# A two-layer graph/FFN kernel on one core: gate, experts and transposes at other steps of the adjacency pass

## What is computed

```python
h = item_feat @ W_item.T + b_item
b = layernorm(x) @ W_user.T + b_user
x = x + relu(adj @ h + b)
xf = layernorm(x)
probs = softmax(xf @ gate_w + gate_b)          # 8 experts
cw = the two largest probs of each row, else 0
for e in range(8):
    y = gelu(xf @ W1[e] + b1[e]) @ W2[e] + b2[e]
    out += cw[:, e:e+1] * y
x = x + out
```

## Time and profile before

| | |
|---|---|
| median of 3 runs | 1682.82 us |
| the profiled execution | 1680.87 us |
| its span, first to last instruction | 1679.0 us |
| TensorE, matmuls | 1617.9 us, 96% of the span |
| TensorE, weight loads | 1314.1 us, 78% |
| VectorE | 1519.5 us, 90% |
| ScalarE | 1257.2 us, 75% |
| Pool | 386.2 us, 23% |
| DMA, mean | 278 GB/s; first fortieth of the span 356 |
| granted TensorE clock | 0.999 |

### The profile page before, as it was taken

One profiled execution on the slowest core, in us unless ns is written; L12 is line 12 of the kernel. 1 busy time (PEld: TensorE's weight loads), 2 busy tenths in 40 slices (PEclk: granted clock), 3 DMA queues, 4 the chain that ended last, 5 costly groups with the idle time before them and its releaser, 6 DMA issues.

```text
span 1679.0 us, 27094 instructions
## 1 busy us (share of the span) xinstructions
PE 1617.9 (96%) x7325; PEld 1314.1 (78%) x7325; DVE 1519.5 (90%) x2164; ACT 1257.2 (75%) x1637; POOL 386.2 (23%) x223
## 2 busy tenths in 40 slices
PE   7999999999999999999999999999999999999997
PEld 6878787878787878787878777777787777787775
DVE  6989999999998989898989898989899999999987
ACT  5777777777777777778687878777777777777765
POOL 1001212222222222131312121313131222221223
PEclk9999999999999999999999999999999999999999
DMA  9998888889897979797979898888888888888852
GB/s 356 341 314 296 274 300 264 302 256 309 252 314 245 317 240 318 249 321 245 319 252 311 263 300 261 298 268 291 274 285 277 289 278 281 286 279 292 271 180 62
DMA packets 148975, 467.06 MB, mean 278 GB/s; under 512 B 16837, under 2 KB 44518, under 8 KB 148954
## 3 DMA queue, kind: packets, MB, share of 16 engines
q1 hardware_dynamic: 144776, 459.00, 82.5%
q10 hardware_dynamic: 3346, 5.51, 0.9%
q0 software_dynamic: 832, 2.30, 0.4%
HBM read 461.30 MB, written 5.44 MB: 278 GB/s over the span
## 4 chain that ended last, share of the span: by engine, by line
PE 53%; DVE 21%; issue 14%; ACT 7%; DMA 3%; DVEq 1%; ACTq 0%; POOL 0%; POOLq 0%; SPq 0%
PE acc L792 12%; PE acc L794 11%; PE acc L793 11%; DVE a_lo L600 9%; ACT a_hi L458 4%; DVE g_lo L709 3%; ACT g_sb L510 3%; PE ps_y L821 2%; PE ps_z L863 2%; PE ps_y L822 2%; PE ps_y L823 2%; PE ps_z L861 2%; PE ps_z L862 2%; DVE t_sb L718 2%; DVE xt_sb L689 2%
## 5 line engine op out<-in xcount | busy, mean ns | idle before, releaser
L600 DVE TENSOR_TENSOR a_lo<-raw,a_hi 128x1000 fp32r<-128x1000 f32 x780 | 922.2, 1206 | 123.8 <-ACT a_hi L458 122.6
L458 ACT ACTIVATE a_hi<-raw 128x1000 fp32r<-128x1000 f32 (+1 forms) x800 | 806.4, 1026 | 225.9 <-PE acc L794 181.4
L792 PE MATMUL acc<-a_hi,h_hi 128*128 128x500 f32 x1560 | 618.4, 396 | 42.2 <-DVE a_lo L600 40.8
L794 PE MATMUL acc<-a_hi,h_lo 128*128 128x500 f32 x1560 | 606.8, 389 | 0.0
L793 PE MATMUL acc<-a_lo,h_hi 128*128 128x500 f32 x1560 | 605.3, 388 | 0.0
L409 POOL TENSOR_TENSOR o_sb<-o_sb,t_sb 128x500 f32<-128x500 f32 x140 | 293.7, 2098 | 535.5 <-DVE t_sb L718 535.1
L792 PEld LDWEIGHTS acc<-a_hi,h_hi 128*128 128x128 f32 x1560 | 293.3, 188 | 131.9 <-DVE a_lo L600 69.9
L794 PEld LDWEIGHTS acc<-a_hi,h_lo 128*128 128x128 f32 x1560 | 293.3, 188 | 60.2
L793 PEld LDWEIGHTS acc<-a_lo,h_hi 128*128 128x128 f32 x1560 | 293.5, 188 | 54.7
L709 DVE TENSOR_TENSOR g_lo<-g_sb,g_hi 128x500 fp32r<-128x500 f32 x320 | 247.8, 814 | 4.0 <-ACT g_hi L516 3.9
L510 ACT ACTIVATE g_sb<-ps_z,b_sb 128x500 f32<-128x500 f32 x320 | 197.5, 668 | 6.5 <-PE ps_z L863 6.2
(11 more groups left out here) (125 smaller groups left out, 1031.6 us busy)
## 6 DMA issues: line engine op xcount, KB each, us to landing
raw<-in_adj_main SPq DMA_DIRECT2D x780, 500.0 KB, 4.8
spread_sb<-scales SPq DMA_DIRECT2D x160, 250.0 KB, 6.3
xr_sb<-in_xR SPq DMA_DIRECT2D x20, 250.0 KB
x_sb<-in_xT SPq DMA_DIRECT2D x20, 250.0 KB, 4.4
out<-o_sb ACTq DMA_DIRECT2D x20, 250.0 KB, 5.9
items<-in_itemT SPq DMA_DIRECT2D x13, 384.0 KB, 8.4
raw<-in_adj_rem SPq DMA_DIRECT2D x20, 156.2 KB, 6.0
g_sb<-in_w POOLq DMA_DIRECT2D x4, 250.0 KB, 6.7
```

What stands on the lines that cost most here:

```text
L458: nc.scalar.activation(a_hi[q][0:rows, 0:cols], raw[s][0:rows, 0:cols], ACT.Copy).then_inc(hi_ready, 1)
L600: nc.vector.tensor_tensor(low, whole, val(high), ALU.subtract).then_inc(lo_ready, 1)
L792: nc.tensor.matmul(acc[:, 0:T], w_hi, m_hi, start=(k == 0), stop=False)
L794: last = nc.tensor.matmul(acc[:, 0:T], w_lo, m_hi, start=False, stop=False)
```

## The change

The computation is the same. Steps of TensorE, ScalarE, VectorE and Pool are renumbered, VectorE's `g_lo` comes 6 instead of 7 steps after the start of an expert, and Pool's steps for the last block get their own table.

```diff
-T_TURN, T_BACK, T_GATE, T_TRANS = 2, 9, 14, 23
-U_TURN, U_DENSE = 35, 38
-STARTS = tuple(range(14, 14 + 5 * E, 5))
-DOWNS = tuple(p + 8 for p in STARTS)
-SCALES = (32, 34, 37, 40, 45, 50, 55, 60)
+T_TURN, T_BACK, T_GATE, T_TRANS = 1, 9, 13, 24
+U_TURN, U_DENSE = 30, 38
+STARTS = (15, 21, 24, 30, 37, 39, 43, 49)
+DOWNS = (21, 28, 35, 38, 43, 45, 51, 55)
+SCALES = (34, 37, 40, 42, 48, 51, 55, 61)
 ADDS = tuple(p + 1 for p in SCALES)
 
-LAST_SCALES = (37, 38, 42, 43, 47, 52, 57, 60)
+LAST_SCALES = (37, 38, 42, 43, 47, 52, 57, 61)
+LAST_ADDS = tuple(p + 1 for p in LAST_SCALES)
 SPREADS = 4
-S_SPREAD = (34, 34, 34, 35, 40, 45, 49, 54)
+S_SPREAD = (34, 34, 34, 35, 42, 45, 49, 54)
 W_SPLIT = 16
 
-A_RELU, A_NORM, A_XN, A_EXP, A_SPREAD, A_SEND, A_STORE, A_USER, A_FFN, A_SCALED = 2, 11, 13, 17, 26, 27, 30, 38, 4, 6
-V_X1, V_STATS, V_NORM, V_LO, V_USTATS, V_UNORM, V_SCALED = 2, 5, 8, 12, 13, 34, 7
-V_LOGITS, V_PROB, V_COMPARE, V_RANK, V_WEIGHT = 16, 18, 20, 21, 22
-P_TAIL, P_USER = 6, 14
+A_RELU, A_NORM, A_XN, A_EXP, A_SPREAD, A_SEND, A_STORE, A_USER, A_FFN, A_SCALED = 2, 13, 15, 17, 27, 28, 30, 38, 4, 6
+V_X1, V_STATS, V_NORM, V_LO, V_USTATS, V_UNORM, V_SCALED = 2, 4, 6, 12, 10, 31, 6
+V_LOGITS, V_PROB, V_COMPARE, V_RANK, V_WEIGHT = 15, 18, 20, 22, 24
+P_TAIL, P_USER = 6, 12
...
+        def adds_at(i):
+            return LAST_ADDS if isinstance(i, int) and i == NB else ADDS
...
-                    if p != ADDS[e]:
+                    if p != adds_at(i)[e]:
```

## The result

The changed kernel takes **1628.19 us** (median of 4 runs, 1627.09 to 1628.92) against 1681.94 us (4 runs, 1679.02 to 1683.05): ratio 0.9682, 95% interval 0.9666 to 0.9699.

The account below looks back on a forecast made before the run. TensorE was taken as the bound, slipping where VectorE's `a_lo` came late. From 1680.9 us, 18 passes at 2.3 less (41.4) and 1 for pass 1, plus 3 for the drain, gave 1641.5, said as 1642; range 1629 to 1664.

Parts of the forecast that it names:

- What bounds the kernel: TensorE, 96% busy, waiting only for `a_lo`: slips before steps 22, 12 and 14 cost 2.66 us of each 81.45 us pass.
- Step 22: TensorE's 1.68 us stall (1.78 with restart) before step 22 goes, by moving the rank and giving step 21 more TensorE work.
- Steps 12 and 14: TensorE's slips there, 0.88 us a pass, go as ScalarE's wait before `xn_hi` falls from 4.32 to some 0.6 us.
- 10: 1.0 (`g_lo` blocked 1.08); 11: ... = -0.3. So TensorE slips 0.3 before step 11: VectorE's lead runs out after Pool blocks `g_lo`; a new TensorE slip before step 11, 0.4 us a pass with restart.
- Rival (a): Pool lets `g_lo` pass at steps 3 and 9: 1635 us, or 1632 with no drain cost; chance 0.2.
- Pool's adds stay at 2.0 to 2.2 us: A sign that the forecast is right: the length of Pool's adds in the profile after the change.
- the ledger: Step-by-step sum of lead, how early VectorE's `a_lo` is done: plus TensorE's step length, less VectorE's work and Pool's block.
- Step 23: VectorE's lead falls to about 0 there, TensorE slips 0 to 0.2 us; 0.2 a pass counted for it and others.
- Pass 1: The pass with half the load, ahead of the 18 alike, gains 1 us.
- Drain: The last block's end gets 3 us longer, bounds 0 and +7, because new queue orders send the weights some 2.7 later.
- T_TURN, U_TURN, the downs beside their `g_lo`, the spread loads, LAST_ADDS: Moved turns, downs sharing a step with `g_lo`, spread loads and Pool's unchanged last-block order: none costs TensorE time.
- The row and the rule: By the issue-order rule step 9's `g_lo` is blocked; by a 3.33 us Pool add it is not, 7 us less.

Follow-up runs that it names:

- a_rank: The changed kernel with V_RANK and V_WEIGHT put back to 21 and 22; 1634.82 us.
- b_norm: The kernel before with only ScalarE's A_NORM and A_XN moved, to 13 and 15 from 11 and 13; 1648.41 us.
- a_more10: The changed kernel with two extra 500-column statistics instructions on VectorE at step 10, their result used nowhere; 1641.52 us.
- b_rank: The kernel before with only the rank and what hangs on it moved one or two steps later (V_RANK 22, V_WEIGHT 24); 1669.41 us.
- b_experts: The kernel before with only the experts' tables of the change, tail and user steps as before; 1677.29 us.
- a_t47: The changed kernel with expert 4's `t_sb` and add one step earlier (SCALES[4] 47 for 48); 1627.77 us.
- b_both: The kernel before with the rank moved (22, weight 24) and A_NORM 13, A_XN 15, the experts left at their steps; 1638.11 us.

## Why the prediction was right and wrong

- **What bounds the kernel: right.** TensorE's slips are the whole difference of the passes. The floor I took was 78.8 from the three slips I added up; 78.43 is reached. I had allowed 0.25 for slips at other steps in the last sum; they were 0.24 at step 7 and some 0.1 in small amounts elsewhere. The passes lost 3.02 us each (81.45 to 78.43), against 2.91 forecast: 0.1 us a pass, 2 us, was missed there.
- **Step 22: right.** The slip went; the lead at 21 was forecast 0.45 and is 0.78, at 22 1.6 and 1.91, at 23 "about 0" and 0.40, at 24 "1.5 and more" and 0.64. a_rank shows the same arithmetic to hold when the rank goes back.
- **Steps 12 and 14: right in mechanism.** The loss at 14, for which no row stood, was 0.44 as at 12. ScalarE's wait before `xn_hi` is 0.8 us a pass (0.6 forecast). Wrong in what it is worth: it also feeds step 22, as b_norm shows (1.53 us a pass instead of 0.88).
- **The step that failed: "10: 1.0 (`g_lo` blocked 1.08); 11: ... = -0.3. So TensorE slips 0.3 before step 11".** Pool's add of expert 4 did not block `g_lo` at step 9; the lead at 10 is 1.97 and at 11 0.80, and the 0.4 at step 11, 18 x 0.4 = 7.2 us, did not come. Rival (a), given 0.2, had this at steps 3 and 9; it came true at 9, while at 3 `g_lo` was blocked. So the sign "Pool's adds stay at 2.0 to 2.2 us" failed too: two of the eight adds of a pass take 4.44 and 3.67. a_more10 shows that the ledger was otherwise sound: about the same time put back by hand brings the slip and 13 us. Why the add waits at one place and not at another is open.
- **Step 23: mis-sized.** The 0.2 a pass for step 23 and others, 3.6 us, did not come either. It had nothing to do with step 9: in a_more10 the leads from step 16 on are those of the changed kernel. The ledger came out 0.2 to 0.4 too low from step 17 to 23.
- **How the sum missed.** Against the 1628.9 of the profiled execution the sum of 1641.5 is 12.6 too high: about 7.2 at step 11, 3.6 at step 23, 2 in the slips of before, 1.9 in pass 1 and 0.4 in pass 0, less 2.7 in the drain. Without that last error the time would lie further out. The range's lower end, 1680.9 - 18 x 2.9 = 1629, took 52.2 off the passes and nothing for pass 1 or the drain; the passes gave 54.3, pass 1 and the drain together 2.8 back, pass 0 another 0.4. The median lies 0.8 below that end.
- **Pass 1: mis-sized.** 1 was forecast, 2.9 came. It has no experts of an earlier block, but it had slips of its own at 6, 9, 12 to 14 and 22, 3.2 us together, and keeps almost none.
- **Drain: mis-sized.** +3 was forecast, +5.7 came, inside its bounds of 0 and 7. The weights were to start 2.7 us later; they start 4.1 later (1598.70 is 27.0 us behind the last relu, against 22.9 before). The queue order that was followed is the one of the trace, but the lower clock, up to 2.3 us ahead of that start, was not in it.
- **T_TURN, U_TURN, the downs beside their `g_lo`, the spread loads, LAST_ADDS: right,** TensorE waits for none of them in passes 2 to 19. Small readings were off without effect: steps 35 to 39 carry four expert halves (35, 37, 38, 39), not five, and the lead into 3 is 2.33, not 2.6; V_LOGITS waits 1.0 us for the gate, not 0.4; ScalarE waits 0.8 for the transposes, not 2.
- **The row and the rule.** I had set the 3.33 us add against the rule of the Trainium skill (SBUF — State Buffer, Who interferes with whom) that VectorE with two SBUF inputs and a GpSimd read exclude each other by issue order. The lock itself is borne out by the blocks of 1.07 to 1.08 us on `g_lo`, `a_lo` and the rank. The order is not: the add started 0.16 us after the first `a_lo` and still let three more instructions go ahead that started later.

## What to carry to other kernels

In a woven schedule keep one number per step, the lead of the feeding engine over the bound one, and add it up from durations in the trace. It was right here within 0.1 to 0.4 us where the blocks were known (b_rank at 22, a_rank, a_more10, most steps of the changed kernel). It missed b_norm by 17 us and b_experts by 24, where ScalarE's late splits set the lead: it needs a line for the third engine as well. Move heavy steps of the feeder to where the bound engine has other work, and look at the waits of the third engine first: the 4.3 us for which ScalarE sat idle looked harmless on an engine that is 75% busy, and taking them away was worth half of what the passes won. What is tuned for the steady loop should be checked in the ramp at its end: steps of its own brought 5 us there.

## What the runs showed of the hardware that was not expected

- An add of Pool of 128x500 that starts 0.16 us after a VectorE instruction with two SBUF inputs does one of two things. Mostly it gets in after that instruction (behind an `a_lo` it takes 2.1 to 2.2 us, and VectorE's next instruction with two SBUF inputs is blocked for 1.07 to 1.08). At some places it lets several instructions with two SBUF inputs go ahead: 4.44 us at step 9 of the changed kernel and 5.56 in a_t47, both until the statistics instructions; 3.67 us behind step 20, until the second part of the rank, which it blocks for 0.95. What decides this is open. In most kernels a place behaves alike in every pass, but in b_both the add at step 21 waits in 5 of 17 passes and blocks in 12, with the same start to 0.01 us. A block is then not certain even at a place where it has been seen.
- In the drain TensorE sat idle 1.00 us, ran eight short matmuls in 1.04, and was idle 1.41 more. Its granted clock was 0.81 from 1584.9 to 1587.4, so it fell in the second idle stretch; it was 0.50 from 1587.4 to 1592.6 and 1.00 again from 1593.6.
